# Second matrix's groups: parts and base weights added by matmuls on TensorE and stored by ScalarE

## What is computed

```python
dWd = ((h_lang @ Wdd.T + bdd) * 0.1).reshape(B, BN, D)     # B, BN, D = 4, 128, 512
dWu = ((h_lang @ Wdu.T + bdu) * 0.1).reshape(B, D, BN)     # Wdd, Wdu: (65536, 128)
down = relu(einsum('bld,bnd->bln', x, Wd + dWd) + bd)      # x: (4, 1024, 512)
up = einsum('bln,bdn->bld', down, Wu + dWu) + bu
out = x + up
```

## Time and profile before

| | us |
|---|---|
| median of 3 runs (lowest to highest) | 220.11 (219.66 to 220.85) |
| the profiled execution's own time | 220.33 |
| its span, first to last instruction | 218.4 |

### The profile page before, as it was taken

The page is one execution under the profiler, slowest core; times in us unless marked ns, Lnnn a source line. Parts: engine busy times, 40 slices in busy tenths (PEclk is TensorE's granted clock), DMA queues, the critical chain, the costliest instruction groups (busy, mean ns, idle before and its releaser), DMA issues.

```text
span 218.4 us, 2995 instructions
## 1 busy us (share of the span) xinstructions
PE 168.3 (77%) x1128; PEld 99.4 (46%) x1128; DVE 167.3 (77%) x103; ACT 52.0 (24%) x92; POOL 61.5 (28%) x41
## 2 busy tenths in 40 slices
PE   1066399677767394995999879998799999999930
PEld 0011163323314041482757438674386554697930
DVE  2865998799999999648486876868799999945840
ACT  2001003111120101150534315443153443441000
POOL 1000000000000000062845347543470787872000
PEclk9996758787969978899999999999999999999995
DMA  5999999999999999999999999999999999995498
GB/s 215 413 366 395 423 422 425 417 426 419 422 423 417 420 390 417 425 425 425 414 425 416 423 425 416 425 414 426 423 414 410 407 399 426 385 345 189 143 340 285
DMA packets 19635, 85.35 MB, mean 391 GB/s; under 512 B 1572, under 2 KB 9768, under 8 KB 10408
## 3 DMA queue, kind: packets, MB, share of 16 engines
q1 hardware_dynamic: 19624, 85.21, 96.7%
HBM read 76.81 MB, written 8.39 MB: 390 GB/s over the span
## 4 chain that ended last, share of the span: by engine, by line
DMA 56%; PE 24%; DVE 14%; issue 1%; SPq 1%; DVEq 0%
DMA w<-in_L_cond_Wdd_dram 30%; DMA w<-in_L_cond_Wdu_dram 27%; DVE wt L265 14%; PE bank L539 13%; PE acc L444 7%; PE dn L519 2%; PE bank L509 1%; PE gt L470 1%; SPq L193 0%; DVE xs L308 0%; SPq L220 0%; DVEq L307 0%
## 5 line engine op out<-in xcount | busy, mean ns | idle before, releaser
L265 DVE STREAM_TRANSPOSE wt<-w 128x2048 f32<-128x2048 f32 x64 | 146.7, 2304 | 32.7 <-DMA w<-in_L_cond_Wdu_dram 20.6
L444 PE MATMUL acc<-wt,st 128*32 128x512 f32 x512 | 74.7, 709 | 38.7 <-DVE wt L265 38.6
L420 POOL TENSOR_TENSOR xs<-xs,bu_all 128x1024 f32<-128x1024 f32 x16 | 37.8, 2362 | 124.7 <-PE bank L509 124.7
L444 PEld LDWEIGHTS acc<-wt,st 128*32 128x32 f32 x512 | 15.4, 121 | 79.4 <-issue 41.6
L519 PE MATMUL dn<-xt,wd_b 128*128 128x256 f32 x128 | 30.6, 382 | 0.0
L539 PE MATMUL bank<-wu_b,down 128*128 128x128 f32 (+1 forms) x192 | 30.4, 313 | 0.0
L539 PEld LDWEIGHTS bank<-wu_b,down 128*128 128x128 f32 x192 | 26.1, 191 | 6.3 <-issue 4.2
L425 POOL TENSOR_TENSOR xs<-up_s,xs 128x512 f32<-128x512 f32 x18 | 22.6, 1280 | 10.7 <-ACT up_s L382 10.7
L519 PEld LDWEIGHTS dn<-xt,wd_b 128*128 128x128 f32 x128 | 23.0, 190 | 3.4 <-issue 0.8
L333 ACT ACTIVATE g_rows<-acc 128x512 f32<-128x512 f32 x16 | 9.6, 600 | 50.9 <-PE acc L444 50.9
L365 ACT ACTIVATE xt<-bank 128x512 f32<-128x512 f32 x32 | 17.4, 595 | 17.6 <-PE bank L509 17.6
(11 more groups left out here) (22 smaller groups left out, 22.3 us busy)
## 6 DMA issues: line engine op xcount, KB each, us to landing
w<-in_L_cond_Wdd_dram SPq DMA_DIRECT2D x32, 1024.0 KB, 7.4
w<-in_L_cond_Wdu_dram SPq DMA_DIRECT2D x32, 1024.0 KB, 10.1
xs<-in_x_dram SPq DMA_DIRECT2D x8, 1024.0 KB, 12.2
out_dram<-xs SPq DMA_DIRECT2D x4, 1024.0 KB, 8.9
out_dram<-xs SPq DMA_DIRECT2D x8, 512.0 KB, 5.4
base_d<-in_L_cond_Wd_dram SPq DMA_DIRECT2D x1, 256.0 KB, 7.1
down<-in_L_cond_bdd_dram SPq DMA_DIRECT2D x1, 256.0 KB, 7.4
down<-in_L_cond_Wu_dram SPq DMA_DIRECT2D x1, 256.0 KB, 11.0
```

Of the source, the lines that this page charges most:

```text
L265: nc.vector.transpose(wt[:, tslot].rearrange("p r (k j) -> p k r j", j=QUAD), w[:, slot, :].rearrange("p (k r h) -> p k r h", r=R, h=QUAD) ...
L420: nc.gpsimd.tensor_tensor(xs[:, b, i0:i0 + UNIT_I], xs[:, b, i0:i0 + UNIT_I], bu_pair, ALU.add).then_inc(bu_added, 1)
L444: last = nc.tensor.matmul(a[TILE * place:TILE * (place + 1)], st[:, r, low * TILE:(low + 1) * TILE], wt[:, slot + h, r], start=low == 0 an ...
```

## The change

Groups of Wdu are now finished as those of Wdd are. `turn_group` holds what was in `turn_down_group`, and `turn_up_group` calls it with the base weights of the second matrix; for each of the 4 blocks there are two matmuls with 64 moving columns in place of one transpose. `store_up_group` on ScalarE stores `gt` to `wu_b` at t % 4 == 3. `add_up_group` is gone from VectorE, with the semaphores `part1_added` and `group_added`; `up_unit` waits for `group_ready` instead. `base_u` now keeps the layout in which a block of 128 of its rows is a stationary operand: it is loaded with "(c d) n -> d c n", which is 4 runs of 512 bytes per partition for Wu and for bdu, where there was 1 run of 2 KB. Its 4 transposes in the second turn, ScalarE's copy of them and the waits on `base_ready` are gone; the first unit of x waits for `base_u_summed`.

```diff
-        base_u = sb("base_u", [P, D])
+        base_u = sb("base_u", [P, C, N])
@@ SP
-                sp.dma_start(wu_nat, Wu.rearrange("(d c) n -> d c n", c=C)).then_inc(base_u_loaded, 16)
-                sp.dma_start(bdu_nat, bdu.rearrange("(d c n) -> d c n", c=C, n=N)).then_inc(base_u_loaded, 16)
+                sp.dma_start(base_u[:], Wu.rearrange("(c d) n -> d c n", c=C)).then_inc(base_u_loaded, 16)
+                sp.dma_start(bdu_nat, bdu.rearrange("(c d n) -> d c n", c=C, n=N)).then_inc(base_u_loaded, 16)
@@ VectorE
-            def add_up_group(g):
-                ...
-                if t % SLOTS == 2 and t > SLOTS:
-                    add_up_group(c // SLOTS - 1)
-            add_up_group(2 * GROUPS - 1)
@@ ScalarE
+            def store_sums(g, total):
+                act.wait_ge(g_turned, g + 1)
+                nc.scalar.activation(total, gt[:, :, 0:PART].rearrange("p c (s b) -> p c s b", b=B), ACT.Copy
+                                     ).then_inc(group_ready, 1)
+            def store_up_group(g):
+                d = slice((g - GROUPS) * D // GROUPS, (g - GROUPS + 1) * D // GROUPS)
+                store_sums(g, wu_b[:, :, d].rearrange("p b (s c) -> p c s b", c=C))
-                    if n == 1 and isinstance(it, int):
-                        act.wait_ge(base_turned, 1)
-                        nc.scalar.activation(base_u[:]..., bank[1][:]..., ACT.Copy).then_inc(base_ready, 1)
+                if t % SLOTS == 3:
+                    store_up_group((CHUNKS + t) // SLOTS)
@@ TensorE
-            def turn_down_group(g, n):
+            def turn_group(g, n, base, select):
                 pe.wait_ge(g_ready, g + 1)
                 if later(g, 1):
                     pe.wait_ge(group_ready, g)
                 for k in range(C):
                     nc.tensor.matmul(gt[:, k, 0:PART], g_rows[:, n, k * P:(k + 1) * P], fold[:],
                                      start=True, stop=False)
+                    last = nc.tensor.matmul(gt[:, k, 0:PART], base(k),
+                                            select(k).unsqueeze(2).to_broadcast([P, SQ, B]),
                                             start=False, stop=True)
                 last.then_inc(g_turned, 1)
             def turn_up_group(g):
-                for k in range(C):
-                    last = nc.tensor.transpose(gt[:, k], g_rows[:, g % 2, k * P:(k + 1) * P], ident[:])
-                last.then_inc(g_turned, 1)
+                first = (g - GROUPS) * D // GROUPS
+                row = first % P
+                pick = ident[:, row:row + D // GROUPS].rearrange("p (s c) -> p c s", c=C)
+                turn_group(g, g % 2, lambda k: base_u[:, first // P], lambda k: pick[:, k])
-                    if u == 6 and isinstance(it, int):
-                        pe.wait_ge(base_u_summed, 1)
-                        for k in range(C):
-                            last = nc.tensor.transpose(bank[1][:, k * P:(k + 1) * P], wu_nat[:, k], ident[:])
-                        last.then_inc(base_turned, 1)
@@ up_unit
-                pe.wait_ge(group_added, cols.stop * GROUPS // D)
+                pe.wait_ge(group_ready, GROUPS + cols.stop * GROUPS // D)
```

More of the change, by code:

```diff
@@ L126, in hyper_adapter @@
         bdd_nat = nat[1].rearrange("p c n -> p (c n)")
-        wu_nat, bdu_nat = nat[2], nat[3]
+        bdu_nat = nat[3]
         acc = [pb(f"acc{n}", [P, COLS]) for n in range(2)]
@@ L148, in hyper_adapter @@
         fold_ready = sem("fold_ready")
-        base_turned = sem("base_turned")
-        base_ready = sem("base_ready")
         wt_ready = sem("wt_ready")
@@ L154, in hyper_adapter @@
         g_turned = sem("g_turned")
-        part1_added = sem("part1_added")
         group_ready = sem("group_ready")
-        group_added = sem("group_added")
         x_turned = sem("x_turned")
@@ L297, in turn @@
                         dve.wait_ge(base_u_loaded, 16 * 4)
-                        nc.vector.scalar_tensor_tensor(wu_nat, bdu_nat, DELTA_SCALE, wu_nat,
+                        nc.vector.scalar_tensor_tensor(base_u[:], bdu_nat, DELTA_SCALE, base_u[:],
                                                        ALU.mult, ALU.add).then_inc(base_u_summed, 1)
@@ L309, in finish_unit @@
                                         ).then_inc(dve_final, 1)
-            dve.wait_ge(base_ready, 1)
             for t in range(CHUNKS):
@@ L335, in copy_group @@
                                      ACT.Copy, scale=DELTA_SCALE).then_inc(g_ready, 1)
+            def store_sums(g, total):
+                act.wait_ge(g_turned, g + 1)
+                nc.scalar.activation(total, gt[:, :, 0:PART].rearrange("p c (s b) -> p c s b", b=B), ACT.Copy
+                                     ).then_inc(group_ready, 1)
             def store_group(g):
[L339 to L342, removed]
+                store_sums(g, wd_b[:, :, :, bass.ds(g * SQ, SQ)].rearrange("p c b s -> p c s b"))
+            def store_up_group(g):
+                d = slice((g - GROUPS) * D // GROUPS, (g - GROUPS + 1) * D // GROUPS)
+                store_sums(g, wu_b[:, :, d].rearrange("p b (s c) -> p c s b", c=C))
             def turn(it):
@@ L348, in turn @@
                         store_group(2 * it + n - 1)
-                    if n == 1 and isinstance(it, int):
-                        act.wait_ge(base_turned, 1)
-                        nc.scalar.activation(base_u[:].rearrange("n (d c) -> n c d", c=C),
-                                             bank[1][:].rearrange("n (c d) -> n c d", c=C), ACT.Copy
-                                             ).then_inc(base_ready, 1)
             turn(0)
@@ L456, in turn_down_group @@
                                      start=True, stop=False)
-                    pick = ident[:, bass.ds(g * SQ, SQ)].unsqueeze(2).to_broadcast([P, SQ, B])
-                    last = nc.tensor.matmul(gt[:, k, 0:PART], base_d[:, k * P:(k + 1) * P], pick,
+                    last = nc.tensor.matmul(gt[:, k, 0:PART], base(k),
+                                            select(k).unsqueeze(2).to_broadcast([P, SQ, B]),
                                             start=False, stop=True)
                 last.then_inc(g_turned, 1)
+            def turn_down_group(g, n):
+                turn_group(g, n, lambda k: base_d[:, k * P:(k + 1) * P],
+                           lambda k: ident[:, bass.ds(g * SQ, SQ)])
             def turn_up_group(g):
[L464 to L468, removed]
-                for k in range(C):
-                    last = nc.tensor.transpose(gt[:, k], g_rows[:, g % 2, k * P:(k + 1) * P], ident[:])
-                last.then_inc(g_turned, 1)
+                first = (g - GROUPS) * D // GROUPS
+                row = first % P
+                pick = ident[:, row:row + D // GROUPS].rearrange("p (s c) -> p c s", c=C)
+                turn_group(g, g % 2, lambda k: base_u[:, first // P], lambda k: pick[:, k])
             pe.wait_ge(st_ready, Q)
@@ L503, in turn_x @@
                 pe.wait_ge(x_loaded[j // PIECE_UNITS], 16)
-                if m < BANK_RING:
-                    pe.wait_ge(base_ready, 1)
-                else:
+                if m == 0:
+                    pe.wait_ge(base_u_summed, 1)
+                if m >= BANK_RING:
                     pe.wait_ge(x_copied, m - BANK_RING + 1)
```

## The result

| | us |
|---|---|
| before, median (lowest to highest) | 219.98 (219.66 to 220.85) |
| after, median (lowest to highest) | 225.83 (225.17 to 226.0) |
| ratio, with its 95% interval | 1.0253 (1.0227 to 1.0279) |
| span of the profiled execution of after | 224.1 (before 218.4) |

The change makes the kernel 5.85 us slower. The prediction said 226.0. The kernel before was run again beside each group of experiments, so its median is 219.98, 220.12 or 220.2 us in what follows. One execution of the kernel with one addition less was in a slower state (240.69 us at a granted clock of 0.76, where all others have 0.89 to 0.94) and is left out.

What follows compares the result with a forecast made beforehand. The prediction took the stream of chunks to bound the kernel up to about 156 us and TensorE after it. Its sum was 220.33 + 5.16 (four late turns) + 0.5 (small packets) = 226.0 us, range 224.7 to 227.7.

Steps and rivals of the forecast that it cites:

- What bounds the kernel: Up to about 156 us the stream of chunks and x sets the pace, then TensorE alone; VectorE is busy but not awaited.
- The turns, 4 x 1.29 = 5.16 us: Second stage on TensorE: turns of groups 12 to 15 go from 0.44 to 1.73 us each, adding 5.16 us.
- The step of every fourth column of the identity: Moving operand of the new matmuls on TensorE: priced the same as neighbouring columns, though no row showed that step.
- A turn costs by its moving columns: Rival on TensorE: 8 x 64 columns equal 4 x 128, so a turn stays 0.44 us; 220.8 us, chance 0.02.
- The early turns, 0: Turns of groups 8 to 11, in the stream-bound stage: TensorE's waits for transposes hide their 1.29 us each, cost 0.
- fifth turn: Rival: lateness from groups 8 to 11 reaches 156.33 and puts 1.29 us more on the path; 227.3 us, chance 0.13.
- VectorE's additions and ScalarE's store, 0 each: Removing 8 times 1.23 us from VectorE gains 0; adding 8 times 0.62 us to ScalarE costs 0.
- Unit 24's finish: Sign near the end of the second layer: it moves from 203.43 to about 209.1.
- Small packets, 0.5: Base-weight loads in the stream-bound stage: 1024 packets of 512 bytes replace 256 of 2 KB, +0.5 us, ends 0 and +1.7.
- 2.0 us to spare: SP's issue queue, 6.48 to 8.48: the longer issuing of the base loads fits in a wait for a transpose.
- The tail gives nothing back: Last eight stores, 12.4 us for 4.2 MB from unit 24's finish: they move whole with TensorE, gain 0.
- the base of 220.33: Time of the profiled execution of the kernel before, to which the terms were added; 0.22 above the median of 220.11.

Runs made afterwards that it cites:

- relief: The changed kernel with groups 8 to 15 turned by 4 transposes each as before, VectorE adding nothing, ScalarE still storing: 220.22 us against 220.12 before.
- Half a turn: The changed kernel without the four matmuls on the base weights in the turns of groups 12 to 15: 222.3 us, ratio to before 1.0095.
- the halves: The changed kernel without the four matmuls on the base weights in the turns of groups 8 to 11: 225.09 us, ratio to before 1.022.
- no_packets: The changed kernel with the loads of Wu and bdu in runs of 2 KB as before: 225.41 us, ratio to before 1.0241.
- reordering: The kernel before with another order of second-layer units at the end, so that unit 24 is finished earlier: 216.27 us against 220.2, ratio 0.9841.
- the reordered changed kernel: The changed kernel with another order of second-layer units at the end, so that unit 24 is finished earlier: 222.06 us, ratio to before 1.0093.
- packets: The kernel before with only the loads of Wu and bdu changed to runs of 512 bytes: 220.15 us against 220.2, ratio 0.9991.

## Why the prediction was right, point by point

- *What bounds the kernel.* Right, and it is what the whole prediction rests on. VectorE's 14.93 of 15 us was no bound: relief gives 220.22 against 220.12. The last pair's 3.8 us behind its transpose was the row that told it.
- *The turns, 4 x 1.29 = 5.16 us.* Right in mechanism, a little small in size (by 0.22 us): between the first pair of the full stage and TensorE's end the trace of after has 5.38 us more, 1.34 per turn. The 0.05 each is the start of the second layer's work behind matmuls instead of transposes. Half a turn measured 0.88 us against 0.87. The step of every fourth column of the identity costs nothing that shows (0.22 us per fp32 matmul, as with neighbours).
- *A turn costs by its moving columns* (the table in "TensorE: Matmul & The Clock Gate" of the Trainium skill, section "Back-to-back issue gap"): this rival fell. It asked for 220.8 us. A transpose with 128 moving columns and a matmul with 64 both take 0.11 us per record.
- *The early turns, 0.* Held within what can be measured (0.2 us by relief, 0.74 for the halves between medians), and by a narrow margin that partly was luck. In after the first weight load of the pair at 156.59 still comes 0.12 us behind the transpose it needs, which ends at 156.47, and no fifth turn is on the path. Of the 1.50 us of idle time ahead of this pair 0.25 are left (0.36 in the weight loads). In no_packets, whose chunk came half a microsecond sooner, none is left: the pair at 156.08 shows no wait. So a stream a little faster would, by this estimate, have put part of an early turn on the path.
- *VectorE's additions and ScalarE's store, 0 each.* Right (relief). Unit 24's finish came where predicted: VectorE's finish at 209.10 against 209.1 predicted, and for ScalarE's 4 us more nobody waits.
- *Small packets, 0.5.* Too high if anything, and not settled: 0.0 between medians in one pair of kernels, with 0.3 at most by its interval, and 0.4 in the other. The step under it that failed is SP's: "2.0 us to spare" was wrong, as one issue took 5.94 us and the next chunk's load left 3.7 us late. What covered it was most likely not SP's time but the loads queued ahead of it.
- *The tail gives nothing back.* Right for this change (8.0 us behind VectorE's last finish in both), and reordering supports the reason: in the kernel before, the reordered one and the changed one the span ends 14.2 us after the first of the eight stores is issued, wherever that is (14.8 in the reordered changed kernel).

The sum by the traces: 5.38 for the turns and 0.29 for the start of the stage, against 5.85 between medians and 5.66 predicted. That the total hits so closely (226.0 against 225.83) is in part luck: the turns were 0.22 too small, the packets' 0.5 is larger than what packets allows, and the base of 220.33 lies 0.35 above the median of 219.98. The 0.29 at the start of the stage is within its scatter and can't be put down to a cause.

## What to carry to other kernels

Of two engines with the same busy share, the one to relieve is the one whose work others wait for: look at the distance between the end of an operation and the start of what reads it (here 3.8 us), and at the chain. Work moved from an engine that runs ahead to one that is full costs its whole duration there. Price it from the same instructions elsewhere in the trace, at the same clock, and look where they stand in time, which decides whether they cost at all (here 1.34 us for a late turn, and by the estimate above some 0.05 for an early one). And where stores end a kernel, look for a window in which the DMA engines move nothing: here 4 us lay there, while taking the additions off VectorE gave nothing that can be measured.

## What was unexpected

- A DMA's issue can take 5.94 us when two loads of 512 runs each stand ahead of it in SP's queue, where it takes 0.44 behind loads of 128 runs. It held the next load back by 3.7 us, with the DMA engines full meanwhile, and packets puts its cost at 0.3 us at most.
- TensorE's granted clock falls to its lower level for some pairs in every trace, the kernel before included, and the length of the wait ahead doesn't order them: 3.40 us behind a wait of 2.88, 3.43 behind 2.27, but 1.92 behind 3.05 and behind 2.31. Ahead of 130 us this costs nothing that shows; on the first pair of the full stage it cost 1.5 us.
- The start of the full stage scatters by up to a microsecond (155.63 to 156.62) between kernels that load the same bytes ahead of it.
